# Two units of a cross-attention kernel moved later within each step of the lead-in

## What is computed

```python
q = heads(hidden_states @ W_q)
k_t = heads(text_ehs @ W_k)
v_t = heads(text_ehs @ W_v)
scores_t = jnp.einsum('bhsd,bhtd->bhst', q, k_t) * attn_scale
probs_t = jax.nn.softmax(scores_t, axis=-1)
text_out = jnp.einsum('bhst,bhtd->bhsd', probs_t, v_t)
...
out = text_out + ip_out
out = out @ W_out + b_out + residual
```

## Time and profile before

| | |
|---|---|
| runs | 2130.80, 2131.04 and 2124.02 us; median 2130.8 |
| the profiled execution | 2125.99 us |
| its span | 2124.2 us, so 1.8 us lie around it |
| matmuls (PE) busy | 2030.1 us, 96% |
| DVE, ACT, POOL busy | 70%, 52%, 22% |
| granted TensorE clock, mean | 0.973 of full |

### The profile page before, as it was taken

One profiled execution on the slowest core, in us unless ns is written; L12 is line 12 of the kernel. 1 busy time (PEld: TensorE's weight loads), 2 busy tenths in 40 slices (PEclk: granted clock), 3 DMA queues, 4 the chain that ended last, 5 costly groups with the idle time before them and its releaser, 6 DMA issues.

```text
span 2124.2 us, 76628 instructions
## 1 busy us (share of the span) xinstructions
PE 2030.1 (96%) x26906; PEld 1739.2 (82%) x26906; DVE 1478.1 (70%) x4447; ACT 1113.0 (52%) x2925; POOL 461.6 (22%) x872
## 2 busy tenths in 40 slices
PE   4899999999999999999999999999999999999975
PEld 3678888888888888888888888888888888888864
DVE  2247777777777777767777776776777677777764
ACT  1355555555555555555555555555555555555531
POOL 1012222221221222222222222222222222222210
PEclk8799999999999999999999999999999999999986
DMA  4111111211111111111111211211111121111000
GB/s 108 48 52 47 49 51 46 55 44 54 48 43 55 47 48 51 48 51 46 54 49 43 56 46 46 54 45 55 44 54 47 43 55 47 48 51 39 25 13 5
DMA packets 108584, 101.44 MB, mean 48 GB/s; under 512 B 42240, under 2 KB 84952, under 8 KB 108184
## 3 DMA queue, kind: packets, MB, share of 16 engines
q1 hardware_dynamic: 104940, 92.88, 16.2%
q10 hardware_dynamic: 3244, 3.33, 0.6%
HBM read 34.13 MB, written 5.41 MB: 19 GB/s over the span
## 4 chain that ended last, share of the span: by engine, by line
PE 93%; issue 2%; DVE 2%; SPq 1%; DMA 1%; ACTq 1%; ACT 1%; POOLq 0%; DVEq 0%; POOL 0%
PE ps_s L761 13%; PE ps_c L836 12%; PE ps_s L792 10%; PE ps_c L903 8%; PE ps_k L663 6%; PE ps_k L856 6%; PE ps_q L740 5%; PE ps_c L892 5%; PE ps_s L808 5%; PE ps_k L688 5%; PE ps_k L861 4%; PE ps_c L869 4%; PE ps_c L908 3%; PE ps_k L691 2%; PE ps_q L822 1%
## 5 line engine op out<-in xcount | busy, mean ns | idle before, releaser
L1145 DVE TENSOR_REDUCE top<-ps_s 128x6 f32<-128x462 f32 (+3 forms) x1024 | 511.2, 544 | 74.2 <-PE ps_s L761 68.5
L1044 ACT ACTIVATE p_t<-ps_s 116x512 f32<-116x512 f32 (+1 forms) x768 | 375.4, 544 | 67.6 <-PE ps_s L792 61.8
L761 PE MATMUL ps_s<-k_blocks,q_sb 32*128 32x231 f32 (+1 forms) x3584 | 323.0, 382 | 17.3 <-issue 15.4
L836 PE MATMUL ps_c<-p_t,v_rows 116*27 116x128 f32 (+1 forms) x7168 | 283.0, 280 | 6.0 <-ACT p_t L1044 5.2
L1370 POOL TENSOR_TENSOR k_blocks<-k_sb,mask_k 128x231 f32<-128x231 f32 x384 | 212.5, 575 | 276.7 <-PE ps_s L792 249.5
L761 PEld LDWEIGHTS ps_s<-k_blocks,q_sb 32*128 32x128 f32 x3584 | 218.4, 185 | 60.9 <-issue 23.4
L1185 DVE TENSOR_TENSOR weighted<-ps_k,probs 128x462 f32<-128x462 f32 (+1 forms) x256 | 142.3, 556 | 177.6 <-PE ps_k L861 175.6
L836 PEld LDWEIGHTS ps_c<-p_t,v_rows 116*27 116x27 f32 (+1 forms) x7168 | 211.0, 107 | 42.3 <-issue 19.8
L792 PE MATMUL ps_s<-q_sb,k_blocks 32*116 32x128 f32 (+1 forms) x5376 | 223.6, 285 | 16.0 <-DVE probs L1160 8.2
L1072 ACT ACTIVATE o_t<-ps_c 128x256 f32<-128x256 f32 x256 | 98.6, 385 | 253.0 <-PE ps_c L892 188.0
L792 PEld LDWEIGHTS ps_s<-q_sb,k_blocks 32*116 32x116 f32 (+1 forms) x5376 | 184.8, 177 | 47.6 <-issue 22.4
(11 more groups left out here) (117 smaller groups left out, 3731.3 us busy)
## 6 DMA issues: line engine op xcount, KB each, us to landing
v_rows<-v_img SPq DMA_DIRECT2D x128, 227.4 KB
context<-in_ctx SPq DMA_DIRECT2D x64, 336.0 KB, 3.1
q_sb<-top_t SPq DMA_DIRECT2D x576, 6.0 KB
v_rows<-v_img SPq DMA_DIRECT2D x64, 115.2 KB
v_rows<-v_img SPq DMA_DIRECT2D x64, 112.2 KB
v_rep<-v_dram SPq DMA_DIRECT2D x64, 50.0 KB
q_sb<-top_t SPq DMA_DIRECT2D x192, 2.0 KB
gram<-g_img SPq DMA_DIRECT2D x64, 46.3 KB
```

What stands on the lines that cost most here:

```text
L761: ins = pe.matmul(ps_s[:, z * 512 + j * GT:z * 512 + j * GT + n], q_sb[c % 3][lo:lo + QUAD, j * S:(j + 1) * S], k_blocks[c % 3][lo:lo + QU ...
L836: ins = pe.matmul(ps_c[t % 2][32 * (g % 4):32 * (g % 4) + UC, g // 4 * S:(g // 4 + 1) * S], v_rows[b % NC][0:n, v:v + UC], p_t[c % 3][0:n, ...
L1044: act.activation(to, source, ACT.Exp, scale=SCALE).then_inc(p_ready, 1)
L1145: dve.tensor_reduce(top[c % 2][:, z * BH:z * BH + m], s.rearrange("p (h t) -> p h t", t=T)[:, :, 0:n], AX.X, ALU.max).then_inc(s_top, 1)
```

## The change

In the lead-in alone (`k is None and t < T0`), PE's `keys` unit of a step with t % 4 == 3 is issued behind `product` and the output's product instead of ahead of them, and PE's `values` is issued behind `turn_back` (and the second Gram wave and a keys unit of t % 4 == 0, which these steps don't have) instead of ahead of `second`. ACT's copies of the two units move to the matching places: keys behind `products`, values behind `exps`. Instruction counts, operands and waits are the same; so is everything from step 20 on. At t = -1 nothing lies between the two places of `values`.

```diff
@@ PE, step
-                if e_keys(t) and t % 4 == 3:
+                filling = k is None and t < T0
+                if e_keys(t) and t % 4 == 3 and not filling:
                     keys(k, t)
                 if exists(t - 2):
                     product(k, t - 2)
...
+                if e_keys(t) and t % 4 == 3 and filling:
+                    keys(k, t)
-                if e_values(t):
+                if e_values(t) and not filling:
                     values(k, t)
...
+                if e_values(t) and filling:
+                    values(k, t)
                 if e_gram(t):
                     image(k, t)
```

## The result

| | before | after |
|---|---|---|
| median of 5 executions | 2126.36 us (2124.02 to 2131.04) | 2138.57 us (2134.55 to 2140.35) |
| the profiled execution | 2125.99 us | 2138.5 us |
| its span | 2124.2 us | 2136.7 us |
| ratio, 95% interval | | 1.0044 (1.0024 to 1.0064) |

By the ratio the change costs about 9.4 us (5.1 to 13.6); the means of the two sets differ by 10.6 us. The median lies at the upper side of the predicted range. The ratio of 0.44% is within the 0.5% that the prediction treats as no change, but its interval leaves no change out: the kernel is slower. The forecast was +5.0 us.

A forecast was written before the change was run, and what follows sets the result against it. PE's own work was taken to bound the kernel; uncovered waits of 0.59 + 0.59 + 0.68 + 1.55 + 1.55 = 4.96, say +5.0 us, on a mean of 2128.0 gave 2133 us, range 2124 to 2142.

The forecast's parts named there:

- What bounds the kernel: Whole kernel: PE's own work bounds it; lead-in delays are not given back, and a new order can only uncover waits.
- The gain at nothing: Lead-in: the output's product ends 1.05 to 2.05 us earlier, but nobody waits for it; 5.5 us slack in step 3.
- the rival that put moved work on somebody's path: Lead-in: x or the exponentials were late after all, up to 6.2 us come back; 2122 us, chance 0.09.
- The rival that nothing is seen: Lead-in: the uncovered waits are given back as delayed work moves behind a fixed clock moment; 2128 us, chance 0.17.
- (a): Steps 3 and 7: values wait for ACT's copy of the keys, +0.59 us in step 3; 0 in 11, 15, 19.
- (b): Gram product waits for ACT's copy of the values: step 7 +0.59 us with the keys' gap, step 11 +0.68.
- (c): Steps 15 and 19: `second` must wait for DVE's subtraction from the scores, +0.47 us each.
- (d): Steps 15 and 19: ACT's text exponentials delay the values' copy, so PE waits 1.08 us instead of 0.64.
- The rule weighed: Uncovered waits: weight loads pulled ahead would each hide one load, sum nearer 4 than 5 us; set aside for the trace.
- The clock rival: Lead-in: waits in steps 11, 15, 19 bring half-clock dips, 4.5 us, plus 1.5 in step 7; 2139 us, chance 0.14.
- Its other part, a rise that comes later in the first steps: Step 7: the clock's rise near 78.4 us comes 3 us later, costing 1.5 us more.
- one of my signs of being wrong: Profile after: clock windows below full between 105 and 125 us or behind 135 would show the forecast wrong.

The follow-up runs named there:

- the keys alone: Against the kernel before, only the keys' unit is moved in the lead-in, values staying ahead of `second`: 2135.92 us, ratio 1.0041.
- the values alone: Against the kernel before, only the first unit of values is moved in the lead-in, keys staying ahead of the product: 2134.02 us, ratio 1.0026.
- the second set's profile of the change: The changed kernel run again with nothing further edited, against the kernel before: 2138.61 us, ratio 1.0048.

## Why the prediction came out as it did

**What bounds the kernel**: right. PE without a gap; a new order could only uncover waits. The loop was untouched, and it has no wait of PE that could take the delay up. The earlier trace rows is a window between two round boundaries; at each of the eight boundaries PE does pause for some 2 us, which I had not looked for, but these pauses were not shorter after (17.4 us in all for 15.4).

**The gain at nothing**: right. In no profile does a step get shorter at full clock; the rival that put moved work on somebody's path (2122 us) is refuted by the keys alone (+8.5) and the values alone (+6.0). The rival that nothing is seen (2128 us) is refuted by the interval of the change, 5.1 to 13.6 us.

**(a)**, said 0.59 in step 3 and (with b) 0.59 in step 7: the wait is 0.59, its cost 0.95 and 0.86. What the sum left out is the restart. The last unit ahead of a wait adds 0.2 to 0.3 us more (2.37 for 2.05, 1.26 for 1.05), the first behind it another 0.06. I priced the wait by the distance from the modelled end of a unit that had been followed at once by others.

**(b)**, said 0.68 in step 11: wait 0.66, cost 0.88, the same restart.

**(c)**, said 0.47 in steps 15 and 19: wait 0.56. DVE's subtraction ended at 141.93 in step 15 and PE began 0.15 us later, where I had counted 0.05.

**(d)**, said a wait of 1.08 instead of 0.64 in these steps: it was 0.66. ACT does run without a pause from the keys' copy to the values', as said. The step that failed is the addition of ACT's durations end to end: consecutive rows of ACT overlap by some 0.1 us (the text exponentials start at 141.97, the keys' copy ends at 142.08), and the four exponentials took 1.90 instead of 1.96, so ACT was free about 0.24 us earlier than I counted, 5.98 us behind the queries instead of 6.22. And PE came to the end of the values 0.17 us later, after the restart of `second`, at 5.93 instead of 5.76. Both took from the wait; the restarts of (c) and (b) put it back into the step: 1.51 us for 1.55. That the step came out so near its forecast is luck: a wait 0.4 us too long and restarts left out cancelled.

**The rule weighed**: the Gram product's weight loads again begin with the first matmul behind the wait (112.63 both in step 11, after 0.86 us without a load):

```profile
112.63 0.35 PEld L717 LDWEIGHTS ps_k<-context 128*77 128x77 f32 x4 [0.86 <-ACT v_img L1014]
```

What the Trainium skill says in "TensorE: Matmul & The Clock Gate", section "Architectural detail: the array is 16× 32×32, not 1× 128×128", of loads pulled ahead of matmuls in flight shows in no wait of this kernel. That a load would also go ahead of a wait was my reading of it, and it is refuted: a wait costs not less than its length but 0.2 to 0.3 us more.

**Sum**: said 5.0, steps measured 5.7, timed 10.6 and 9.8. Beyond the waits there are 4 to 5 us, of which about 2 are seen as clock in the profiles, and the clock of the timed executions has room for all of them. The forecast put this term at nothing. The clock rival priced it at 6 us, and its 2139 us is what was measured (2138.6), but it put the clock's cost in the wrong place: it put dips behind the waits of 11, 15 and 19, and there is none behind 15 and 19, and none in the loop but at the boundaries of its rounds, where the kernel before has them too. Its other part, a rise that comes later in the first steps, is part of what happened. And one of my signs of being wrong came true, a clock below full between 105 and 125 us. In the profile after it fell at 121 us (window, us, PE busy, granted clock, DMA):

```profile
122.00:124.00 2.00, 2.00 (x14) 0.50 0.05 14
```

Before, it fell at 126 us; in the second set's profile of the change it fell at 130 us. I had given the whole of it a chance of 0.14, by the argument that the 0.64 us gap of step 7 had brought no dip. That argument looked at what follows one wait. What the profiles show lies in the stretches of the lead-in that run partly at half clock anyway, steps 3 to 8 and 12 to 14, and there a shift of the work goes with more of it.

**The level**: centring on 2128.0 for the kernel before was fair, its later means were 2127.7 to 2128.4. 2133 lacked the restart (0.7) and the excess (4 to 5); the median of 2138.6 is within the range because the range took in the clock case, and not by the terms of the sum, whose upper bound of 7 us the timed difference passed.

## What to carry to other kernels

An order in which PE never waits has its buffers' copies covered by other units; a unit moved to stand directly ahead of the reader of its copy costs the whole copy, 0.6 us here, plus 0.2 to 0.3 us for draining and restarting PE. Price such a move by the distance between two landmarks around it in the trace, not by the gap alone, and count what every queue holds ahead of the copy. And where the stretch in question runs partly at a lower clock, repeat the profile before reading differences of a few microseconds: two profiles of the kernel before differ there by 3.5 us between the scores of pairs 0 and 8.

## What the runs showed of the hardware

The clock's record is not to be trusted ahead of its first change. In the first profile of the change the window 50 to 60 us reads full clock, and in its second profile (the change once more) it reads half:

```profile
50.00:60.00 10.00, 8.73 (x44) 1.00 0.00 0
```

```profile
50.00:60.00 10.00, 8.73 (x42) 0.50 0.00 0
```

Yet PE was busy for the same 8.73 us, and the matmuls of the values took 1.78 us for four in both, about twice what they take at full speed (0.92 in step 11). The durations of equal instructions tell the clock where the record doesn't. The Trainium skill's statement that I cited, that the point of the clock's change varies from run to run ("TensorE: Matmul & The Clock Gate", section "Part 1: The HAM clock gate (the "warmup" mystery)"), agrees with the runs: in two profiles of the kernel before the clock rose again at 57.9 and at 50.8 us. Between kernels, too, the first rise is at 27 us in the profile before and not in the profile after, where the same instructions of the values, ahead of everything that the change delays, take 0.98 and 1.78 us:

```profile
27.29 0.98 PE L688 MATMUL ps_k<-wv,context 128*77 128x224 f32 x4 [0.66 <-ACT v_img L1009]
```

```profile
27.33 1.78 PE L688 MATMUL ps_k<-wv,context 128*77 128x224 f32 x4 [0.66 <-ACT v_img L1014]
```

And the loop itself, 1682 to 1692 us in the thirteen profiles of unchanged loops, holds between 3.4 and 23.9 us at half clock. Every such stretch begins within 1.6 us of a boundary of the hardware loop's rounds, where PE pauses some 2 us each time and waits for nothing that the profile shows (8 times, 17.4 us in the profile after). With a spread of 9 us over these profiles, against 5 in the last steps, the loop is a large part of what makes executions of one kernel differ.
